# Routed expert outputs written to their own rows and added on chip, in place of adding them up in DRAM

## What is computed

```python
x = x + tanh(g_xattn[0]) * L0_xattn(layernorm(x), ctx, ctx)      # gated recurrent cell
xf = layernorm(x)
logits = xf @ router_w.T + expert_bias                            # 8 experts
rw, sel = top_k(logits, 2); rw = softmax(rw)                      # two experts for each token
x = x + tanh(g_ffn[0]) * (shared_ffn(xf) + sum_k rw[k] * expert_ffn[sel[k]](xf))
x = x + tanh(g_xattn[1]) * L1_xattn(layernorm(x), ctx, ctx)       # softmax attention, 16 heads
x = x + tanh(g_ffn[1]) * L1_ffn(layernorm(x))                     # 16 experts, top 4, and a shared one
```

## Time and profile before

| | us |
|---|---|
| median of 3 runs (878.46 to 878.55) | 878.5 |
| the profiled execution | 878.5 |
| its span, first to last instruction | 876.7 |
| mean granted TensorE clock, share of full | 0.963 |
| routed tiles, one tile | 5.49 |

### The profile page before, as it was taken

One profiled execution on the slowest core, in us unless ns is written; L12 is line 12 of the kernel. 1 busy time (PEld: TensorE's weight loads), 2 busy tenths in 40 slices (PEclk: granted clock), 3 DMA queues, 4 the chain that ended last, 5 costly groups with the idle time before them and its releaser, 6 DMA issues.

```text
span 876.7 us, 14796 instructions
## 1 busy us (share of the span) xinstructions
PE 775.0 (88%) x5188; PEld 603.1 (69%) x5188; DVE 507.9 (58%) x1186; ACT 392.6 (45%) x805; POOL 227.2 (26%) x208
## 2 busy tenths in 40 slices
PE   4456389999998999999998888996788999999997
PEld 3345277788886777777776545655567888888886
DVE  5477866465454333333333488879766665756644
ACT  5468555244342222222222478878655434243322
POOL 0079110026703222222222328575310000000000
PEclk9787879999999999999999999999899999999999
DMA  8347752015252333333335510101004005050130
GB/s 304 116 188 273 243 199 84 1 25 193 86 192 54 49 50 49 49 49 49 49 49 139 170 65 13 74 13 74 1 1 98 1 3 120 1 122 1 43 80 25
DMA packets 37478, 74.44 MB, mean 85 GB/s; under 512 B 4416, under 2 KB 25536, under 8 KB 35648
## 3 DMA queue, kind: packets, MB, share of 16 engines
q1 hardware_dynamic: 30256, 64.16, 22.8%
q0 software_dynamic: 7152, 9.34, 6.8%
HBM read 59.76 MB, written 19.01 MB: 90 GB/s over the span
## 4 chain that ended last, share of the span: by engine, by line
PE 60%; DVE 11%; ACT 6%; issue 4%; DMA 4%; DVEq 3%; SPq 0%; POOLq 0%; ACTq 0%
PE t_y_ps L2172 7%; PE t_up L2154 7%; PE f_y L1726 4%; PE a_turned L968 4%; PE a_score L946 3%; PE a_score L948 3%; PE a_score L947 3%; DMA sums<-t_y,t_dest 3%; PE a_turned L872 2%; PE a_proj L845 2%; PE t_gate L2146 2%; PE t_gate L2147 2%; PE t_gate L2145 2%; PE t_h_turned L2161 2%; PE f_gate L1707 1%
## 5 line engine op out<-in xcount | busy, mean ns | idle before, releaser
L2123 POOL DMA_INDIRECT sums<-t_y,t_dest x39 | 60.8, 1559 | 161.0 <-DVEq L2245 142.2
L2204 ACT CAST t_xT_hi<-t_x_turned 128x256 fp32r<-128x256 f32 x39 | 14.5, 372 | 151.4 <-PE t_x_turned L2136 151.4
L2172 PEld LDWEIGHTS t_y_ps<-W,t_hidT 128*128 128x128 f32 x312 | 59.2, 190 | 25.2 <-issue 19.2
L2172 PE MATMUL t_y_ps<-W,t_hidT 128*128 x312 | 73.8, 379 | 0.8 <-ACT t_hidT L2214 0.8
L2154 PE MATMUL t_up<-W,t_xT 128*128 x156 | 73.4, 593 | 0.0
L1134 ACT CAST a_hhi<-a_hid 128x512 fp32r<-128x512 f32 x48 | 29.8, 620 | 78.3 <-DVEq L1420 76.7
L1422 DVE TENSOR_TENSOR a_hlo<-a_hid,a_hhi 128x512 fp32r<-128x512 f32 x48 | 33.2, 692 | 35.1 <-ACT a_hhi L1134 35.1
L1123 ACT ACTIVATE a_act_g<-a_score 128x512 f32<-128x512 f32 x48 | 28.6, 597 | 55.1 <-PE a_score L948 54.9
L2233 DVE TENSOR_TENSOR t_hid<-t_act_g,t_up 128x512 f32<-128x512 f32 x39 | 26.8, 687 | 36.1 <-ACT t_act_g L2209 34.2
L801 POOL TENSOR_TENSOR a_sc<-a_sc,a_nmx 128x512 f32<-128x512 f32 x32 | 33.3, 1041 | 54.6 <-DVE a_nmx L1268 54.6
L1083 ACT ACTIVATE a_pr<-a_sc,a_nmx 128x128 f32<-128x128 f32 x128 | 40.8, 391 | 13.4 <-DVE a_nmx L1268 12.7
(11 more groups left out here) (393 smaller groups left out, 2157.7 us busy)
## 6 DMA issues: line engine op xcount, KB each, us to landing
W<-in_w_dram SPq DMA_DIRECT2D x9, 1536.0 KB, 8.4
a_cb<-comb_rows SPq DMA_DIRECT2D x16, 512.0 KB, 8.1
W<-m_rows SPq DMA_DIRECT2D x14, 512.0 KB, 4.7
slot_tokens<-in_blank_rows_dram SPq DMA_DIRECT2D x1, 5031.0 KB, 22.9
t_x<-slot_tokens SPq DMA_DIRECT2D x39, 129.0 KB, 2.6
a_raw<-in_w_dram SPq DMA_DIRECT2D x3, 1536.0 KB, 6.2
X<-in_x_dram SPq DMA_DIRECT2D x4, 512.0 KB, 5.8
ctxT_all<-in_ctxT_dram SPq DMA_DIRECT2D x4, 512.0 KB, 9.1
```

The source lines that it names most:

```text
L2123: pool.indirect_dma_start(sum_dram, bass.IndirectOffsetOnAxis(ap=dest[p][:, 0:1].bitcast(U32), axis=0), y[p][:], None, compute_op=ALU.add) ...
L2172: last = pe.matmul(y_ps[p][:, 0:D], hidT[p][:, h], W[:, ds(e, 1), at:at + D], start=(h == 0), stop=(h == HT - 1))
```

## The change

The routed outputs get a row of their own for each token and choice: the DRAM tensor `outputs` has 2 x 2048 rows for tokens, and one for each of the 4992 slots, to which blank slots go. The indirect DMA writes plainly and does not add, and a send no longer waits for the send before it. X stays on the chip, so the four stores to `sums` and the blanking of its spare rows go.

At the start of the attention SP loads both rows of each token, `picked`, chunk by chunk (8 transfers of 512 KB in place of 4 into X). DVE adds the two halves of chunk 0 to X (`add_first`); POOL adds those of chunks 1 to 3, in pieces of two sequences (12 additions of 128x512), after DVE's first, and raises `picked_added` once a chunk. `statistics2(c)` waits for that.

The orders at the start of the attention change as well. On DVE, `keep((0, "x", 1))` goes ahead of `keep((1, "v", 0))` and `statistics2(1)`; the statistics of chunks 2 and 3 go from ahead of the loop to behind soft(0), and their `scale2` behind the first half of soft(1). On ACT the early root of line 1139 goes, both `keep((1, "k", n))` come ahead of `deviation2(0)`, `keep((0, "q", n))` ahead of `normalise2(1)`, and `deviation2(2)` and `deviation2(3)` go to the end of step s = 0.

```diff
@@ cell @@
             sp.dma_start(xg_dram.rearrange("(p i) d -> p (i d)", p=128),
                          blank_rows.rearrange("(p i) d -> p (i d)", p=128)).then_inc(slots_blank, 16)
-            sp.dma_start(sum_dram[T:T + 128, :], blank_rows[0:128, 0:D]).then_inc(sums_blank, 16)
@@ attention_tiles @@
+        with ExitStack() as place:
+            sb("picked", [128, 2, B, D], F32, place)
@@ attention_feed_forward @@
-        by_dve = [(0, "v", 0), (0, "v", 1), (1, "v", 0), (0, "x", 1), (1, "v", 1)]
+        by_dve = [(0, "v", 0), (0, "v", 1), (0, "x", 1), (1, "v", 0), (1, "v", 1)]
...
             for p in range(2):
                 sp.wait_ge(y_stored[p], 16 * ((NT + 1 - p) // 2))
+            rows = y_dram[0:2 * T, :].rearrange("(k s p) d -> p k s d", k=2, s=B)
             for c in range(NCH):
                 part = slice(c * CH, (c + 1) * CH)
-                sp.dma_start(X[:, part, :], sums[:, part, :]).then_inc(x_loaded[c], 16)
+                for k in range(2):
+                    sp.dma_start(picked[:, k, part, :], rows[:, k, part, :]).then_inc(picked_loaded[c], 16)
...
             penalties(0)
             penalties(1)
+            pool.wait_ge(first_added, 1)
+            for c in range(1, NCH):
+                pool.wait_ge(picked_loaded[c], 32)
+                for half in range(2):
+                    at = slice(c * CH + 2 * half, c * CH + 2 * half + 2)
+                    for k in range(2):
+                        last = pool.tensor_tensor(X[:, at, :], X[:, at, :], picked[:, k, at, :], ALU.add)
+                        if k == 0:
+                            pool.drain()
+                last.then_inc(picked_added, 1)
             pool.wait_ge(rw_loaded, 32)
...
-            act.activation(largest[:, 0, 0:1], cst[:, C_EPS:C_EPS + 1], ACT.Sqrt)
-
             for p in range(2):
                 act.wait_ge(y_stored[p], 16 * ((NT + 1 - p) // 2))
-            keep((1, "k", 0))
+            for n in range(2):
+                keep((1, "k", n))
             deviation2(0)
             normalise2(0)
-            keep((1, "k", 1))
             keep((0, "x", 0))
             deviation2(1)
+            for n in range(2):
+                keep((0, "q", n))
             normalise2(1)
-            keep((0, "q", 0))
-            deviation2(2)
-            keep((0, "q", 1))
-            deviation2(3)
...
                 if s >= 1:
                     keep_out(s - 1)
+                if s == 0:
+                    deviation2(2)
+                    deviation2(3)
...
+            def add_first():
+                dve.wait_ge(picked_loaded[0], 32)
+                for k in range(2):
+                    last = dve.tensor_tensor(X[:, 0:CH, :], X[:, 0:CH, :], picked[:, k, 0:CH, :], ALU.add)
+                    if k == 0:
+                        dve.drain()
+                last.then_inc(first_added, 1)
+                dve.drain()
+
             def statistics2(c):
-                dve.wait_ge(x_loaded[c], 16)
+                wait(dve, picked_added, c)
...
             for n in range(2):
                 keep((0, "v", n))
+            add_first()
             statistics2(0)
             scale2(0)
             normalise2(0)
-            keep((1, "v", 0))
+            keep((0, "x", 1))
+            for n in range(2):
+                keep((1, "v", n))
             statistics2(1)
-            keep((0, "x", 1))
-            keep((1, "v", 1))
             scale2(1)
             normalise2(1)
-            for c in (2, 3):
-                statistics2(c)
-            for c in (2, 3):
-                scale2(c)
             for s in range(B + 2):
...
                 if s >= 2:
                     finish(s - 2)
+                if s == 1:
+                    scale2(2)
+                    scale2(3)
                 if s in (1, CH + 1):
                     normalise2(s // CH + 2)
                 if s < B:
                     soft(s, 1)
+                if s == 0:
+                    statistics2(2)
+                    statistics2(3)
@@ shared_feed_forward @@
-            def store(c):
-                sp.wait_ge(y_free, 2 * c + 2)
-                sp.dma_start(sums[:, c * CH:(c + 1) * CH, :], X[:, c * CH:(c + 1) * CH, :]).then_inc(x_stored[c], 16)
-
...
-            store(0)
-            store(1)
...
-            store(2)
@@ routed_tiles @@
                 sp.dma_start(x[p][:], xg_dram[ds(i * 128, 128), :]).then_inc(x_loaded[p], 16)
-                if i == 1:
-                    sp.wait_ge(y_free, 2 * NCH)
-                    sp.dma_start(sums[:, (NCH - 1) * CH:, :], X[:, (NCH - 1) * CH:, :]).then_inc(x_stored[NCH - 1], 16)
...
                 pool.wait_ge(y_ready, i + 1)
-                wait(pool, y_stored[1 - p], 16 * ((i + 1) // 2))
                 pool.sem_inc(sent, 1)
-                pool.indirect_dma_start(sum_dram, bass.IndirectOffsetOnAxis(ap=dest[p][:, 0:1].bitcast(U32), axis=0), y[p][:],
-                                        None, compute_op=ALU.add).then_inc(y_stored[p], 16)
-            pool.wait_ge(sums_blank, 16)
-            for c in range(NCH):
-                pool.wait_ge(x_stored[c], 16)
+                pool.indirect_dma_start(y_dram, bass.IndirectOffsetOnAxis(ap=dest[p][:, 0:1].bitcast(U32), axis=0), y[p][:],
+                                        None).then_inc(y_stored[p], 16)
@@ program, blank_rows, kernel @@
-    sum_dram = nc.dram_tensor("sums", (T + 128, D), F32, kind="Internal").ap()
+    y_dram = nc.dram_tensor("outputs", (2 * T + NT * 128, D), F32, kind="Internal").ap()
...
-    rows[:, D] = (T + np.arange(NT * 128, dtype=np.int32) % 128).view(np.float32)
+    rows[:, D] = (2 * T + np.arange(NT * 128, dtype=np.int32)).view(np.float32)
...
-        ("token_homes", _np.tile(_np.arange(T, dtype=_np.int32).reshape(1, B, 128), (2, 1, 1)).transpose(2, 0, 1)),
+        ("token_homes", _np.arange(2 * T, dtype=_np.int32).reshape(2, B, 128).transpose(2, 0, 1)),
```

30 lines of the change are left out of this document (13 added, 17 removed).

## The result

The changed kernel takes 885.1 us (median of 7 runs, 881.3 to 890.2), before 878.5; the ratio is 1.0076 with an interval of 1.0045 to 1.0105. I had forecast 881.0 and a range up to 884.0, so slower was the right side and the size was wrong: +6.6 in place of +2.5. The 7 runs of before lie within 2.2 us and those of the changed kernel within 9, but that is no mark of the change: 31 later runs of before lie within 8.4.

The account below looks back on a forecast made before the run. PE has most to do, so time can be won only where it waits, at the ends of the routed-tile stage. Terms -0.9 -1.1 -4.3 +1.4 +2.6 +1.0 -0.55 +3.5 +0.9 gave +2.5: 878.5 to 881.0 us, range 876.5 to 884.0.

Follow-up runs that it names:

- shared, stat. early: Changed kernel with DVE adding chunks 0 and 1, POOL 2 and 3; statistics of chunk 2 before the loop, chunk 3 in soft(0), roots before the first exponential: ratio 1.0086.

## What to carry to other kernels

Work that an engine did while it waited is free only there: before moving it, ask whether its new place has a gap on that engine, and price the engine's side and the other engine's side apart, for the longer counts. When work is put on an idle engine, read its idle stretch in the trace for "issue" pauses too; the pause came with the second such instruction whatever that was, and what is put there has to bear it. A term read off one trace of the kernel before may be a matter of that run: take a second trace before pricing it. And a gain ahead of a stage is worth what the new first input of the stage leaves of it: here 6 us of quicker sends paid for twice the loads and the additions, and the best arrangement came out level.

## Of the hardware, not expected

- POOL's second two-operand instruction after the mask products comes 3.33 or 3.34 us late in each of the twenty traces, be it an addition of 128x512, a product of 128x16 or the second piece of the router weights (128x32). In three kernels two small products took the pause while POOL had nothing else to do.
- Beside additions by POOL, DVE's normalisation (0.73 us) takes up to 2.1 us more, while DVE's statistics keep their 1.4 us and POOL's addition its 1.26. Where DVE adds at the same time (the kernel "shared, stat. early"), both are held: DVE's pair takes 3.42 us for 2.52, and single additions by POOL 1.86 and 2.25.
- A plain indirect send of 128 rows of 1 KB takes POOL 0.96 us and lands in 2.4, a summing one 1.56 and 3.9 (medians of 39).
- The spread of a kernel's runs goes with its mean granted clock: 0.48 us for each 0.001 over the 29 runs of the change (correlation -0.90). In runs of before the tie is looser, 0.21 to 0.64 us with correlations of -0.32 to -0.83. The mean is 0.960 to 0.962 before and 0.955 to 0.956 after.
